# A scan whose steps share TensorE with the products around it: four layers on one core, and the end of the program rewritten

## The chip, the core and the metric

The kernel runs on one core of a Trainium2 chip. TensorE (PE, with its weight loads as PEld) multiplies and transposes, VectorE (DVE), ScalarE (ACT) and GpSimd (POOL) do the rest, and SyncE (SP) issues the DMAs. All data are fp32; a product shows in the records as two passes, each with its own weight load, a transpose as one. The metric is the device time of one execution in microseconds (us), median of the runs.

## What is computed

Sixteen sequences of 128 tokens with 256 features go through four layers, each with its own weights. The reference, cut to what matters here:

```python
x = L0(x, ctx, mask)      # self attention with a mask, gated memory, feed-forward (relu)
x = L1(ctx, x)            # two single-head attentions, a small feed-forward (gelu), norms
x = L2(x, ctx)            # causal cross attention, norm, feed-forward (gelu)
# L3:
x = x + mha(norm(x), norm(base_state))
U = (norm(x) @ W_in.T + b_in) @ Bmat                  # [16, 128, 64]
def step(s, u_t):
    s = silu(s @ A.T) + u_t                           # s: [16, 64]
    return s, s
_, states = scan(step, zeros, U)                      # 128 steps, one after another
x = x + states @ Cmat
mod = program_probs.mean(axis=1) @ W_prog.T + b_prog
return x + mod[:, None, :]
```

The scan is serial in the tokens: step t needs the state of token t-1, for all sixteen sequences together.

## The kernel before

The sixteen sequences are taken in pairs, so there are eight tiles (`NT = 8`) of 2 x 128 tokens. Each tile goes through streams of work named by a letter: H and A are layer 0, G the context, M layer 1, J and B layer 2, K and C layer 3. The order in which TensorE, VectorE, ScalarE and GpSimd take the steps of all streams is written out by hand in four long lists (`TENSOR_ORDER` and so on, in which `C7.mix` is the step "mix" of stream C for tile 7). The lists are the same in both kernels.

TensorE's results go round four PSUM banks (`work_bank_0` to `_3`). A step that fills a bank counts up the semaphore `filled`; the engine that empties it counts up that bank's `drained`. `open_bank` waits until the bank's last user has been emptied. Attention scores go to four more banks (`scores_bank`), which the waits on `maxed` and `exped` free.
The last steps of the main part are a chain for tile 7: `C7.turn` (transposes of attention weights), `C7.mix`, `C7.out` (L545), addition and norm on VectorE and GpSimd, `C7.flip.x7` (four transposes, L528), `C7.drive` (L723), which leaves the inputs of the scan in `u_all` [64, 128 tokens, 16 sequences].

Then comes the end of the program, which the change rewrites:

- TensorE first runs four products of the matrix A with all of `u_all` (L731), 32 tokens each, into the four scores banks: the silu of step t needs A times (silu state of t-1 plus u of t-1), and this is the second part of it.
- Sixteen products of one column (L739) give the means of the program probabilities, loaded into `prog` when `C7.drive` is done.
- For t = 2 to 127 a product of 64 rows, 64 columns of weights and 16 moving columns (L744) adds A times the state to the bank, and ScalarE writes the silu to `w_state` (L1126). They wait for each other in each step through `stepped` and `silued`.
- VectorE builds `stT`, whose upper half holds the means for all tokens (L1021) and whose lower half is silu plus u, 32 tokens at a time (L1029), the last quarter in four pieces.
- Sixteen products of 256 columns (L754) multiply `stT` with `w_last` (Cmat over W_prog), two to a bank; VectorE adds each bank to `x7` (L1038) and SyncE stores the pair (L495).

`stT`, `prog` and the hidden rows of the feed-forwards (`hT`) are one piece of memory, `hidden`; `w_state` lies in `probs`.

## Time and profile before

| | us |
| --- | --- |
| median of 3 runs | 937.99 (936.37 to 939.94) |
| profiled execution, its own time | 936.61 |
| its span | 934.5 |
| TensorE busy | 765.0 (82%) |
| VectorE, ScalarE, GpSimd busy | 550.1, 443.9, 336.5 |
| mean granted clock of TensorE | 0.907 of 2.4 GHz |
| start of the first wide product of the end (L731) | 827.81 |
| first and last product of the scan (L744) start | 838.27 and 920.77 |

A profile is one execution. Its span runs from the first to the last instruction, and its own time is 2.1 us longer. Lines of the page give an instruction group by source line, with busy time, mean length, and the idle time of its engine just before. The chain of waits goes back from the last instruction to what released each piece of work. Busy time of TensorE is no measure of its throughput, since its records overlap.

### The profile page before, as it was taken

The numbers are of one execution on the slowest core, as the hardware profiler recorded it, in microseconds if no ns is written. First come the engines' busy times: TensorE is split into PE (matmuls) and PEld (weight loads), VectorE is DVE, ScalarE is ACT, GpSimd is POOL, SyncE is SP. The second block draws the span as 40 slices with busy tenths as digits, with TensorE's granted clock in tenths as the row PEclk, the third lists the DMA queues.
The fourth block names the chain that finished last, engine by engine and source line by source line (L and its number), as shares of the span: only waits on it lengthen the run. The fifth ranks groups of instructions, "written<-read, shape, count | busy, mean of one in ns | idle before, by whom it ended". The sixth has DMA issues, their size and how long they took to land.

```text
span 934.5 us, 16718 instructions
## 1 busy us (share of the span) xinstructions
PE 765.0 (82%) x5520; PEld 617.2 (66%) x5520; DVE 550.1 (59%) x2244; ACT 443.9 (48%) x1776; POOL 336.5 (36%) x343
## 2 busy tenths in 40 slices
PE   0479798799899989998999999999889667575556
PEld 0368677688677868787787778877678546434445
DVE  0267767745977687678867885878763661320002
ACT  0184275536583667366536845683723631312221
POOL 3032444433644454354525551655343331200000
PEclk9999999899999999999999999999999888655556
DMA  8400100000000000000000000000000000010002
GB/s 321 156 7 2 29 1 18 13 1 1 13 7 12 2 12 7 13 13 2 7 13 12 1 1 13 2 1 1 2 1 1 1 1 1 1 22 1 1 0 90
DMA packets 14710, 18.75 MB, mean 20 GB/s; under 512 B 3485, under 2 KB 12194, under 8 KB 13986
## 3 DMA queue, kind: packets, MB, share of 16 engines
q1 hardware_dynamic: 14626, 17.69, 5.7%
q8 instruction: 45, 0.74, 0.3%
q14 instruction: 39, 0.32, 0.1%
HBM read 15.59 MB, written 2.10 MB: 19 GB/s over the span
## 4 chain that ended last, share of the span: by engine, by line
PE 60%; DVE 18%; ACT 10%; issue 6%; SPq 2%; POOL 2%; DMA 2%; DVEq 0%; POOLq 0%
PE work_bank L536 19%; PE work_bank L545 18%; ACT probs L1063 6%; PE scores_bank L744 5%; PE work_bank L674 4%; DVE probsT L985 3%; PE scores_bank L572 3%; DVE xn L902 3%; ACT probs L1126 3%; PE work_bank L594 2%; DVE stats L921 2%; PE work_bank L528 2%; DVE probs L884 2%; DMA bias<-in_mask 2%; PE work_bank L666 1%
## 5 line engine op out<-in xcount | busy, mean ns | idle before, releaser
L767 POOL TENSOR_TENSOR probs<-probs,rtotal 128x512 f32<-128x512 f32 x160 | 165.6, 1044 | 209.9 <-DVE rtotal L975 208.3
L1063 ACT ACTIVATE probs<-probs,nmx 128x128 f32<-128x128 f32 x512 | 197.9, 390 | 54.8 <-DVE nmx L884 54.5
L545 PE MATMUL work_bank<-L_w,hidden 128*128 128x256 f32 x512 | 114.8, 383 | 1.6 <-issue 1.0
L985 DVE COPY probsT<-work_bank 128x512 f32<-128x512 f32 x160 | 104.7, 681 | 11.5 <-PE work_bank L674 10.6
L767 POOL TENSOR_TENSOR rstd<-veps,half 128x2 f32<-128x2 f32 x64 | 44.8, 699 | 184.7 <-DVE veps L929 183.8
L545 PEld LDWEIGHTS work_bank<-L_w,hidden 128*128 128x128 f32 x512 | 97.2, 192 | 15.2 <-issue 1.6
L674 PE MATMUL work_bank<-ident,probs 128*128 128x128 f32 x640 | 94.1, 287 | 15.9 <-POOL probs L767 9.9
L674 PEld LDWEIGHTS work_bank<-ident,probs 128*128 128x128 f32 x640 | 73.8, 146 | 36.3 <-POOL probs L767 19.3
L1063 ACT ACTIVATION_READ_ACCUMULATOR probs<-probs,nmx 128x1 f32 x512 | 96.6, 189 | 0.0
L528 PE MATMUL work_bank<-ident,xn 128*128 128x128 f32 x256 | 42.6, 287 | 48.0 <-DVE xn L902 45.9
L744 PE MATMUL scores_bank<-probs,a_t 64*64 64x16 f32 x252 | 49.5, 275 | 33.4 <-ACT probs L1126 33.4
L884 DVE CUSTOM_DVE_ANT_0 probs<-scores_bank,causal 128x128 f32<-128x128 f32 x256 | 56.2, 285 | 20.6 <-PE scores_bank L572 20.0
L536 PE MATMUL work_bank<-B_actT,L_w 128*128 128x256 f32 x256 | 63.9, 403 | 5.3 <-DVE probsT L985 3.6
L528 PEld LDWEIGHTS work_bank<-ident,xn 128*128 128x128 f32 x256 | 30.0, 147 | 57.0 <-issue 49.1
L744 PEld LDWEIGHTS scores_bank<-probs,a_t 64*64 64x64 f32 x252 | 36.1, 202 | 46.7 <-ACT probs L1126 46.7
L884 DVE CUSTOM_DVE_ANT_0 probs<-scores_bank,bias 128x128 f32<-128x128 f32 x256 | 57.5, 283 | 7.8 <-PE scores_bank L572 7.5
L536 PE MATMUL work_bank<-A_actT,L_w 128*128 128x256 f32 x256 | 61.3, 390 | 0.0
L536 PEld LDWEIGHTS work_bank<-B_actT,L_w 128*128 128x128 f32 x256 | 50.2, 201 | 15.3 <-DVE B_actT L945 7.4
L536 PEld LDWEIGHTS work_bank<-A_actT,L_w 128*128 128x128 f32 x256 | 48.7, 195 | 8.6 <-issue 1.7
L1126 ACT ACTIVATE probs<-scores_bank 64x16 f32<-64x16 f32 x127 | 22.6, 178 | 62.4 <-PE scores_bank L744 62.4
L1029 DVE TENSOR_TENSOR hidden<-probs,u_all 64x128 f32<-64x128 f32 (+1 forms) x7 | 4.2, 641 | 78.6 <-ACT probs L1126 78.6
L1063 ACT ACTIVATE probs<-scores_bank,nmx 128x128 f32<-128x128 f32 x128 | 45.0, 390 | 6.8 <-DVE nmx L877 6.8
(162 smaller groups left out, 1424.9 us busy)
## 6 DMA issues: line engine op xcount, KB each, us to landing
L_w<-in_L_w SPq DMA_DIRECT2D x4, 1024.0 KB, 10.8
x_in<-in_x SPq DMA_DIRECT2D x8, 256.0 KB, 2.7
c_in<-in_ctx SPq DMA_DIRECT2D x8, 256.0 KB, 2.7
out<-x_all SPq DMA_DIRECT2D x8, 256.0 KB, 2.2
rows<-in_rows SPq DMA_DIRECT2D x1, 1280.0 KB, 8.0
bias<-in_mask SPq DMA_DIRECT2D x8, 128.0 KB, 2.2
L_wq<-in_L_wq SPq DMA_DIRECT2D x3, 256.0 KB, 9.7
L_wv<-in_L_wv SPq DMA_DIRECT2D x3, 256.0 KB, 10.2
```

Source lines behind the costliest of these rows:

```text
L528: mm = nc.tensor.transpose(d[:, c * PT + b * P:c * PT + b * P + P], src[:, b, c * P:c * P + P], ident[:])
L536: mm = nc.tensor.matmul(d[:, m * PT:m * PT + PT], w[:, k, (m0 + m) * P:(m0 + m) * P + P], xT[:, k, :], start=(k == 0), stop=(k == DC - 1))
L545: mm = nc.tensor.matmul(d[:, b * D:b * D + D], xT, w, start=(n == 0), stop=(n == len(todo) - 1))
L572: mm = nc.tensor.matmul(s_bank[g][:, c * 2 * P:(c + 1) * 2 * P], qT[s][of, c, b * P:b * P + P], kT[s][of, c, b].rearrange("p e t -> p (e t ...
L674: mm = nc.tensor.transpose(d[:, j * P:j * P + P], src[:, j, :], ident[:])
L744: mm = nc.tensor.matmul(s_bank[t // 32][0:SS, (t % 32) * B:(t % 32) * B + B], a_t[:], w_state[:, t - 1, :], start=False, stop=True, skip_g ...
L767: return nc.gpsimd.tensor_tensor(out, a0, a1, op)
L884: ins = nc.vector.tensor_tensor_reduce(out=e_at[slot][:, j, :], in0=d[:, j * P:j * P + P], in1=more, scale=-1.0, scalar=3.0e38, op0=ALU.ad ...
L902: nc.vector.tensor_scalar(norm_slot(s, i, key)[:, b, :], src[:, b, :], moments[:, n, b, 0:1], rstd[:, n, b:b + 1], ALU.subtract, ALU.mult) ...
L985: nc.vector.tensor_copy(turn_slot(s, i, key), d[:].rearrange("p (j k) -> p j k", j=4))\
L1063: ins = nc.scalar.activation(e_at[slot][:, j, :], src, ACT.Exp, bias=nmx[:, slot, j:j + 1], scale=1.0 if s == "C" else -1.0, accum_out=tot ...
L1126: nc.scalar.activation(w_state[:, t, :], s_bank[t // 32][0:SS, (t % 32) * B:(t % 32) * B + B], ACT.Silu)\
```

## The change

1. **Waits.** TensorE's waits go through a helper `ready`, which leaves out a wait that an earlier one of the same semaphore already covers. Where a step waited for several emptied banks, it waits only for the last one that each of VectorE and ScalarE empties (`emptied_last`).
2. **Means.** The sixteen mean products stand ahead of `C7.flip.x7` and go to a scores bank; their load is issued when the last feed-forwards have been read, and VectorE copies them after the last `flip`. The Silu table is loaded by a Silu of zeros after `C7.out`.
3. **Wide products.** Only the first stands ahead of the scan. The others stand behind steps 8, 40 and 72.
4. **The first 96 tokens** (`EARLY`) of each sequence are multiplied in halves of 128 columns (`early_part`), 32 products in all. From step 99 (`FROM`) on, one stands behind each step; three are left for after the scan. VectorE adds them two sequences at a time, and SyncE stores them so.
5. **The last 32 tokens** of four sequences are multiplied side by side in four 32-column tiles of the array. In steps 12 to 19 that is done with u and the means (`late_part`), and after the last step once more with the silu states read straight from `w_state`. Four DMAs move the residual of these tokens to `late`, where the four sequences of a group lie under each other; four DMAs store them, two from SyncE and two from ScalarE.

```diff
+EARLY, FROM = 96, 99
+        def emptied_last(fills):
+            out = []
+            for e in "da":
+                mine = [x for x in fills if x in EMPTIED[e]]
+                if mine:
+                    s, i, step = max(mine, key=EMPTIED[e].get)
+                    out.append(done(s, i, *step))
+            return out
...
-            sp.wait_ge(*done("C", NT - 1, "drive"))
+            sp.wait_ge(*filled_at("A", NT - 1, "ffn2"))
+            sp.wait_ge(*filled_at("B", NT - 1, "ffn2"))
             sp.dma_start(prog, a["prog"].rearrange("b s k -> s b k")).then_inc(prog_loaded, 16)
-            for j in range(NT):
-                sp.wait_ge(last_added, j + 1)
-                sp.dma_start(out[bass.ds(j * PAIR, PAIR)].rearrange("b s d -> s b d"), x7(j)).then_inc(out_stored, 16)
-            sp.wait_ge(out_stored, 16 * NT)
+            sp.wait_ge(*summed_at("C", NT - 1, "x7b"))
+            for j in range(4):
+                sp.dma_start(late[32 * j:32 * j + 32, :, :],
+                             x7_all[EARLY:P, :, :].rearrange("p (g j) d -> p g j d", j=4)[:, :, j, :])\
+                    .then_inc(late_moved, 16)
+            for n in range(NT):
+                sp.wait_ge(last_added, n + 1)
+                sp.dma_start(out[bass.ds(n * PAIR, PAIR), 0:EARLY].rearrange("b s d -> s b d"), x7(n)[0:EARLY])\
+                    .then_inc(out_stored, 16)
+            for j in (0, 1):
+                sp.wait_ge(late_added, 4)
+                sp.dma_start(out[:, EARLY:P].rearrange("(g j) s d -> j s g d", j=4)[j], late[32 * j:32 * j + 32])\
+                    .then_inc(out_stored, 16)
...
+            def ready(of, n):
+                if waited.get(of.name, 0) < n:
+                    waited[of.name] = n
+                    pe.wait_ge(of, n)
...
             def mix(s, i, step):
                 first = 4 * (step[1] if len(step) > 1 else 0)
-                for j in range(4):
-                    pe.wait_ge(*done(s, i, "turn", first + j))
-                pe.wait_ge(*done(KEYS[s], i, "v"))
+                for at in emptied_last([(s, i, ("turn", first + j)) for j in range(4)]):
+                    ready(*at)
+                ready(*done(KEYS[s], i, "v"))
...
+                if (s, i, step) == ("C", NT - 1, ("flip", "x7")):
+                    ready(exped, EXPED["C", NT - 1, ("exp", 3)])
+                    pe.wait_ge(prog_loaded, 16)
+                    for b in range(B):
+                        mm = nc.tensor.matmul(s_bank[3][SS:P, b:b + 1], prog[:, b, :], mean_w[:], start=True, stop=True)
+                    mm.then_inc(prog_meant, 1)
...
+            def late_part(k):
+                g, lo = k // 2, (k % 2) * P
+                for j in range(4):
+                    mm = nc.tensor.matmul(w_bank[g // 2][32 * j:32 * j + 32, (g % 2) * D + lo:(g % 2) * D + lo + P],
+                                          stT[:, 4 * g + j, EARLY:P], w_last[:, lo:lo + P], start=True, stop=True)
+                if k % 4 == 3:
+                    mm.then_inc(late_filled, 1)
+
+            def early_part(k):
+                b, lo = k // 2, (k % 2) * P
+                n = b // PAIR
+                if k % 4 == 0:
+                    if n < 2:
+                        pe.wait_ge(states_ready, 3)
+                    elif n < 4:
+                        pe.wait_ge(late_added, n - 1)
+                    else:
+                        pe.wait_ge(last_added, n - 3)
+                at = (b % PAIR) * D + lo
+                mm = nc.tensor.matmul(w_bank[(n + 2) % W_BANKS][0:EARLY, at:at + P], stT[:, b, 0:EARLY],
+                                      w_last[:, lo:lo + P], start=True, stop=True)
+                if k % 4 == 3:
+                    mm.then_inc(last_filled, 1)
...
-            for n in range(4):
+            mm = from_u(0)
             for t in range(1, P):
...
                 if t > 1:
                     pe.wait_ge(silued, t - 1)
                     mm = nc.tensor.matmul(s_bank[t // 32][0:SS, (t % 32) * B:(t % 32) * B + B], a_t[:],
                                           w_state[:, t - 1, :], start=False, stop=True, skip_group_check=True)
                 mm.then_inc(stepped, 1)
+                if t in (8, 40, 72):
...
+                    from_u(t // 32 + 1)
...
+                if 12 <= t < 20:
+                    late_part(t - 12)
+                if t >= FROM:
+                    early_part(t - FROM)
+
+            pe.wait_ge(silued, P - 1)
+            for g in range(4):
+                for j in range(4):
+                    mm = nc.tensor.matmul(s_bank[g // 2][32 * j:32 * j + 32, (g % 2) * D:(g % 2) * D + D],
+                                          w_state[:, EARLY:P, 4 * g + j], w_last[0:SS, :], start=True, stop=True)
+                if g % 2:
+                    mm.then_inc(late_filled, 1)
+            for k in range(P - FROM, 2 * B):
+                early_part(k)
```

How the instructions stand on the engines, first of the kernel before, then of the changed one. TensorE from `C7.mix` to the first scan steps, before; the names in brackets are the semaphores waited for:

```order
L594 MATMUL work_bank<-probsT,v 32x128 [waits drained_3,drained_2,drained_0,drained_1]
L594 MATMUL work_bank<-probsT,v 32x128 x15
L545 MATMUL work_bank<-L_wo,C_qT 128x256 [waits drained_1,drained_0]
L545 MATMUL work_bank<-L_wo,C_qT 128x256 x3
L528 MATMUL work_bank<-ident,xn 128x128 [waits normed,drained_2]
L528 MATMUL work_bank<-ident,xn 128x128
L528 MATMUL work_bank<-ident,xn 128x128 [waits normed]
L528 MATMUL work_bank<-ident,xn 128x128
L723 MATMUL work_bank<-C_actT,w_drive 64x256 [waits drained_3,drained_2]
```

```order
L731 MATMUL scores_bank<-u_all,a_t 64x496 [waits drained_3]
L731 MATMUL scores_bank<-u_all,a_t 64x512 x3
L739 MATMUL work_bank<-mean_w,hidden 64x1 [waits drained_3,drained_2,prog_loaded,drained_1,drained_0]
L739 MATMUL work_bank<-mean_w,hidden 64x1 x15
L744 MATMUL scores_bank<-probs,a_t 64x16 [waits silued] x126
```

The same stretch of TensorE in the changed kernel, up to the first late products:

```order
L629 MATMUL work_bank<-probsT,v 32x128 [waits drained_0,drained_3]
L629 MATMUL work_bank<-probsT,v 32x128 x15
L580 MATMUL work_bank<-L_wo,C_qT 128x256 [waits drained_1,drained_0]
L580 MATMUL work_bank<-L_wo,C_qT 128x256 x3
L664 MATMUL scores_bank<-mean_w,hidden 64x1 [waits prog_loaded,exped]
L664 MATMUL scores_bank<-mean_w,hidden 64x1 x15
L563 MATMUL work_bank<-ident,xn 128x128 [waits normed,drained_2]
```

```order
L772 MATMUL scores_bank<-u_all,a_t 64x496 [waits drained_3]
L806 MATMUL scores_bank<-probs,a_t 64x16 [waits silued] x7
L772 MATMUL scores_bank<-u_all,a_t 64x512
L806 MATMUL scores_bank<-probs,a_t 64x16 [waits silued] x4
L779 MATMUL work_bank<-w_last,hidden 32x128 [waits drained_3,drained_2,late_ready,drained_1,drained_0]
L779 MATMUL work_bank<-w_last,hidden 32x128 x3
L806 MATMUL scores_bank<-probs,a_t 64x16 [waits silued]
L779 MATMUL work_bank<-w_last,hidden 32x128 x4
```

The mean products have moved ahead of the transposes, three wide products into the scan, and `mix` waits for two semaphores instead of four.

TensorE from step 126 of the scan to the end of the program in the changed kernel:

```order
L806 MATMUL scores_bank<-probs,a_t 64x16 [waits silued]
L796 MATMUL work_bank<-w_last,hidden 96x128
L806 MATMUL scores_bank<-probs,a_t 64x16 [waits silued]
L796 MATMUL work_bank<-w_last,hidden 96x128 [waits last_added]
L825 MATMUL scores_bank<-w_last,probs 32x256 [waits silued]
L825 MATMUL scores_bank<-w_last,probs 32x256 x15
L796 MATMUL work_bank<-w_last,hidden 96x128 x3
```

Before, the scan's 126 products stood in a row and sixteen products of 256 columns behind them (L754, two for each wait); now one of 128 columns stands behind each of the last steps, and sixteen quarter-tile products and three of 128 columns behind the scan.

## Rows read from the trace of the kernel before

**Rows 1.** The page: granted clock in 40 slices, chain by engine, one costly group.

```profile
PEclk9999999899999999999999999999999888655556
...
PE 60%; DVE 18%; ACT 10%; issue 6%; SPq 2%; POOL 2%; DMA 2%; DVEq 0%; POOLq 0%
...
L744 PE MATMUL scores_bank<-probs,a_t 64*64 64x16 f32 x252 | 49.5, 275 | 33.4 <-ACT probs L1126 33.4
```

**Rows 2.** The chain that ended last, in order of time: start, length, what.

```profile
827.81 7.03 PE scores_bank L731 x8
834.84 3.50 PE work_bank L739 x32
838.35 0.33 PE scores_bank L744 x2
...
920.77 0.41 PE scores_bank L744 x2
...
921.92 9.27 PE work_bank L754 x32
931.21 0.69 DVE x_all L1038
```

**Rows 3.** Timeline of one scan step: start, length, engine, line, what, idle before.

```profile
871.93 0.28 PEld L744 LDWEIGHTS scores_bank<-probs,a_t 64*64 64x64 f32 x2 [0.38 <-ACT probs L1126]
871.93 0.39 PE L744 MATMUL scores_bank<-probs,a_t 64*64 64x16 f32 x2 [0.27 <-ACT probs L1126]
872.36 0.18 ACT L1126 ACTIVATE probs<-scores_bank 64x16 f32<-64x16 f32 x1 [0.48 <-PE scores_bank L744]
872.59 0.29 PEld L744 LDWEIGHTS scores_bank<-probs,a_t 64*64 64x64 f32 x2 [0.37 <-ACT probs L1126]
```

**Rows 4.** Stretches: length, busy PE, PEld, DVE, ACT, POOL, clock, DMA share, GB/s.

```profile
827.80:838.20 10.40, 10.39 (x40) 5.07 (x40) 0.00 (x0) 1.68 (x3) 0.00 (x0) 0.50 0.24 50
...
921.90:926.10 4.20, 4.17 (x10) 3.36 (x11) 1.81 (x5) 0.00 (x0) 0.00 (x0) 0.50 0.09 31
926.30:931.20 4.90, 4.88 (x23) 3.96 (x21) 3.56 (x6) 0.00 (x0) 0.00 (x0) 1.00 0.70 232
```

**Rows 5.** Timeline of TensorE's products, tile 7 of layer 3.

```profile
813.01 1.93 PE L594 MATMUL work_bank<-probsT,v 128*32 128x128 f32 x32 [1.09 <-DVE probsT L985]
815.75 3.78 PE L545 MATMUL work_bank<-L_wo,C_qT 128*128 128x256 f32 x8 [0.80 <-DVE C_qT L991]
823.09 1.09 PE L528 MATMUL work_bank<-ident,xn 128*128 128x128 f32 x4 [3.56 <-DVE xn L902]
```

**Rows 6.** DMA: two issues in a row on SyncE's queue, and one load.

```profile
3.15 0.43 SPq L467 DMA_DIRECT2D L_wv<-in_L_wv  x1
3.63 0.43 SPq L467 DMA_DIRECT2D L_wk<-in_L_wk  x1
...
hidden<-in_prog SPq DMA_DIRECT2D x1, 512.0 KB, 4.2
```

**Rows 7.** Timeline of VectorE in the scan.

```profile
838.59 1.22 DVE L1021 COPY hidden<-means 64x2048 f32<-64x2048 f32 x1
858.05 1.01 DVE L1029 TENSOR_TENSOR hidden<-probs,u_all 64x512 f32<-64x512 f32 x1 [18.23 <-ACT probs L1126]
```

**Rows 8.** Timeline of TensorE's weight loads where the tile shape changes.

```profile
832.93 0.23 PEld L731 LDWEIGHTS scores_bank<-u_all,a_t 64*64 64x64 f32 x1 [0.63 <-issue]
834.77 3.49 PEld L739 LDWEIGHTS work_bank<-mean_w,hidden 128*64 128x64 f32 x32 [1.61 <-issue]
```

**Rows 9.** Wait instructions of open_bank; stalls of mix; pieces of the chain at three stalls.

```profile
L503 PEldq EVENT_SEMAPHORE  x461: 51/51/3605, 38.3 to 823.3; - x154
...
  DVE probsT L985: 28.2, 12
...
423.08 0.14 issue
...
812.66 0.35 issue
...
815.71 0.04 issue
```

More of the change, by code:

```diff
@@ L253 @@
 FILL_AT = {x: n for n, x in enumerate(FILLS)}
+EMPTIED = {e: {x: n for n, x in enumerate(program(e)) if x in FILL_AT} for e in "da"}
 ROUND_AT = {x: n for n, x in enumerate(ROUNDS)}
@@ L511, in flip @@
                 elif key == "x4":
-                    pe.wait_ge(*done("M", i, "self"))
+                    ready(*done("M", i, "self"))
                     src = x4[:, i % 2]
                 elif key == "o":
-                    for b in range(PAIR):
-                        pe.wait_ge(*done("B", i, "mix", b))
+                    for at in emptied_last([("B", i, ("mix", b)) for b in range(PAIR)]):
+                        ready(*at)
                 else:
@@ L1024, in _ @@
[L1024 to L1033 removed]
+            nc.vector.tensor_copy(stT[SS:P, :, :], means[SS:P, :].unsqueeze(2).broadcast_to([SS, B, P]))
@@ new lines, in _ @@
+            dve.wait_ge(*done("C", NT - 1, "drive"))
+            nc.vector.tensor_copy(stT[0:SS, :, EARLY:P], u_all[:, EARLY:P, :].rearrange("p t b -> p b t"))\
+                .then_inc(late_ready, 1)
+            for k in range(2):
+                dve.wait_ge(late_filled, k + 1)
+                if k == 0:
+                    dve.wait_ge(late_moved, 16 * 4)
+                nc.vector.tensor_tensor(late[:, 2 * k:2 * k + 2, :], by_batch(w_bank[k]), late[:, 2 * k:2 * k + 2, :],
+                                        ALU.add).then_inc(late_added, 1)
@@ new lines, in add_late @@
+            def add_late(k):
+                dve.wait_ge(late_filled, k + 3)
+                if k == 0:
+                    dve.wait_ge(late_added, 2)
+                nc.vector.tensor_tensor(late[:, 2 * k:2 * k + 2, :], by_batch(s_bank[k]), late[:, 2 * k:2 * k + 2, :],
+                                        ALU.add).then_inc(late_added, 1)
+            whole = (P - FROM) // 4
+            for n in range(whole):
+                add_early(n)
+            for k in range(2):
+                add_late(k)
@@ L1040, in _ @@
+            for n in range(whole, NT):
+                add_early(n)
         @block.scalar
@@ L1120, in _ @@
                     ins.then_inc(free, 1)
[L1122 to L1123 removed]
+            act.wait_ge(*filled_at("C", NT - 1, "out"))
+            nc.scalar.activation(w_state[:, 0, :], zero[:], ACT.Silu)
             for t in range(1, P):
@@ L1127, in _ @@
                     .then_inc(silued, 1)
+            for j in (2, 3):
+                act.wait_ge(late_added, 4)
+                nc.scalar.dma_start(out[:, EARLY:P].rearrange("(g j) s d -> j s g d", j=4)[j],
+                                    late[32 * j:32 * j + 32]).then_inc(out_stored, 16)
 def _columns(inputs):
```

123 lines of the change are left out of this document (57 added, 66 removed).

## The prediction

> **What bounds the kernel now.** I read the page first: its chain of waits, its clock row, then the chain in order of time for the last 110 us. TensorE heads 60% of the chain, and its granted clock is 9 tenths or more until it falls to 5 for the last eighth of the program [rows 1]. That last part is the scan, and the chain in order of time shows what it is made of [rows 2]. After the last input of the scan is ready (827.8), TensorE runs four products of 496 or 512 columns (7.03 us) and sixteen products for the mean of the program probabilities (3.50 us), and only then the scan's second step begins, at 838.3. The last step begins at 920.77, 82.5 us later. Then come sixteen products of 256 columns (9.27 us), whose eight additions and stores run alongside, the last addition at 931.21, and the last store, with which the span ends at 934.5. One scan step takes 0.66 us [rows 3]: TensorE's loads start at 871.93, its product ends 0.39 later, ScalarE's Silu runs from 872.36 for 0.18, and the next load starts at 872.59. Nothing in a step is throughput. Its loads take 0.28 and its products are 16 columns wide, so the array itself is free some 0.15 to 0.2 us after the start and lies idle for half a microsecond. The change tries to fill that hole. All of it runs at 1.2 GHz, as the granted clock of 0.50 says [rows 4].
>
> **Terms of the sum, head.** The first step needs only the first of the four wide products, 7.03 / 4 = 1.76 us; with its latency and one Silu, the second step can start at about 827.81 + 1.9 + 0.25 = 829.98 instead of 838.35 - 0.08 = 838.27. That is -8.3 us. It needs the sixteen mean products out of the way. They now stand ahead of the last transposes of the main part, after the product that ends the attention. That product's eight records of 256 columns start at 815.75 and take 3.78, so the array is free at 819.2; the transposes start at 823.09 because VectorE and GpSimd normalise in between [rows 5]. The mean products need 3.50 in a hole of 3.9, less a change of shape of 0.14 (below): they fit by about 0.26 us. If they did not, the transposes and all behind them would move by the overshoot; I take 0, at most +0.3. Their input, a load of 4.2 us to landing [rows 6], is now issued right after the last feed-forward product instead of at the scan's start. VectorE's small copy of the means sits in its idle time before the last drive term. The copy of the means over all tokens (1.22 us) and the new copy of the inputs (like an addition of 64x512, 1.01 us) [rows 7] end at about 830.2, and the first late product waits for them only at step 12, about 837.
>
> **Wide products in the scan.** Three of 512 columns now stand behind steps 8, 40 and 72, same array shape as the step. Each streams 1.71 us (0.85 for a record, two records), from about 0.25 after the step's start, so the next step starts at about 1.97 instead of 0.66: 3 x 1.31 = +3.9 us. So of the 5.3 us removed ahead of the scan, 3.9 come back.
>
> **Products of another shape in the scan.** Here the price is in what TensorE does when the tile shape changes. In the wide products the loads run one ahead of the products, one each 0.85 us. The load at 832.93 is the last of them; its product starts one record later, at 833.79, and streams until 834.64. The next load, for a 128x64 tile after 64x64 ones, is not taken ahead and comes only at 834.77 [rows 8]: a change of shape costs 0.13 after the end of the stream, and the load ahead is lost. Each inserted product changes shape twice, since the step is 64x64, the late products 128x32 and the early ones 128x128 tiles. The Trainium skill says the same in "TensorEngine Tiling (Array Packing)", Key Properties: changing the tiling mode, not just the tile, drains the engine. It speaks against this change, and the price here is taken from the rows alone.
>
> An **early step** (steps 99 to 127, 29 products of 128 columns with 96 rows of output): the step's second record starts at 0.13 (0.39 [rows 3] less a record's 0.26 to 0.28 [rows 1]), the shape has changed at 0.30, the load and the first start-up take 0.06 to 0.13, two records stream 0.213 each (half of the 0.43 for 256 columns, from 3.78 for eight [rows 5]), and the change back takes 0.14. The next step starts at 0.93 to 1.03. I take 1.00, nearer the upper end because the group of eight records [rows 5] shows 0.16 of start-up beyond its eight streams and the latency. That is +0.34 on each of 28 intervals: +9.5 us (7.6 to 10.4). The bound below is 0, if the product fitted the hole; it is a real bound, as the hole is 0.5 wide and the product's stream 0.43.
>
> A **late step** (12 to 19, eight groups of four 32-column tiles): the mix product shows four such tiles at work together, 32 records of 128 columns in 1.93 [rows 5], so a group of eight records streams 0.43, with 0.05 of stagger. The next step starts at about 0.92: 8 x 0.26 = +2.1 us. VectorE's early additions, 0.69 each [rows 2], come once in four steps and wait for nobody on the path.
>
> **Tail.** Now from the start T of the last step. Before, the last addition starts at T + 10.44 and the span ends at T + 13.7. After: the early product of that step and the change of shape until T + 1.02; sixteen products of 64x32 tiles, four at a time, 256 columns, 4 x 0.85 = 3.41 and another change of shape until T + 4.6; the three early products that are left over, 6 x 0.213 with start-up and latency until T + 6.3; one addition of 0.69: T + 7.0. Then SyncE issues three stores, where before it issued one; back to back they start 0.47 apart with cold queues [rows 6], about 0.42 at the 0.37 that stores take, so the end comes 2.6 + 0.8 = 3.4 after the addition: T + 10.4. That is -3.3 us.
>
> **Waits.** The helper `ready` drops waits that an earlier one covers; the built program has 262 wait instructions on TensorE instead of 680 (461 of the old ones are those of one line, `open_bank`) [rows 9]. A wait instruction costs 0.05 and stands 0.1 before the next. While the array is busy the sequencer runs ahead and it costs nothing. Where TensorE stands still for the result, it costs: with three of them the mix starts 0.35 after the copy it waited for, with one 0.14, with none 0.04 [rows 9]. The mix's loads stood still for that copy 12 times: 12 x 0.3 = 3.6. Some 25 other stalls lose one wait each: 25 x 0.08 = 2.0. Ceiling 5.6; floor 0, since no wait is added there (VectorE, ScalarE or GpSimd may be what is late next). TensorE heads 60% of the chain, so I take 0.6 x 5.6 = -3.5.
>
> **Sum:** -8.3 + 3.9 + 9.5 + 2.1 - 3.3 - 3.5 = +0.4 us on a span of 934.5 in a run of 936.6. The three timed runs have a median of 938.0, 1.4 above it; I add the sum to the median: **938.4 us**. What the head and the tail give, the steps in the scan take back.
>
> **Rivals.** (1) *The clock rises in the early steps.* TensorE will have no idle gap for 29 us. For it: in the tail of before it was busy without a gap at 0.50 from 921.9, and the clock was 1.00 from 926.3 on [rows 4]. Against it: from 827.8 to 838.2 it was busy all the time too, and stayed at 0.50 [rows 4]; those were 64x64 and 128x64 tiles, the tail's were 128x128. In an early step the 128x128 tiles stream for 0.43 of 1.0. At 2.4 GHz the inserted product fits the hole: -9.5, and the end's streams halve, -2.5: 926.4. The Trainium skill's "TensorE: Matmul & The Clock Gate", Why this matters for your kernels, advises to leave no idle gaps to stay at full clock; the row from 827.8 shows that this is not enough here. (2) *The early product mostly hides* in the Silu's time, because its load is taken ahead after all, or the waits give their whole ceiling: -5 to -9: 931. (3) *Slower: a full drain on each change of shape.* The step's product has a latency of 0.39, of which I let only 0.30 pass before the next shape's load, and after the early product 0.14 instead of the 0.2 or more of a record's latency. With 0.11 more on each of two changes in 36 steps: 72 x 0.11 = +8: 946. It decides from an early step of about 1.15 us upwards. (4) *The waits bring nothing*, because another engine is late next: +3.5: 941.9, still no difference. (5) *The quarter tiles do not run side by side* with these operands: +1.3 in each of 8 late steps and +10 in the tail: 959.
>
> **How the numbers follow.** A measurement of this kernel can tell about 0.5%, 4.7 us, from no change. Forecast 0.47 (a small part of it below 933.3), rival 1 0.10, rival 2 0.10, rival 3 0.15, rival 4 0.15, rival 5 0.03. Faster by over 0.5%: 0.10 + 0.10 + 0.02 = 0.22. Within: 0.45 + 0.15 = 0.60. Slower: 0.15 + 0.03 = 0.18. The range leaves out rivals 1 and 5 and the far part of 3: 928.0 to 946.5.
>
> **What would show it.** The second step starts 2.2 us after the first wide product does; the transposes before the last drive term start within 0.3 us of when the normalised rows are ready; steps 20 to 98 stay at 0.66; steps with a wide product take 1.97, late steps 0.92, early steps 1.00 at a granted clock of 0.50; from the last step's start to the end 10.4 us; up to the last drive term the program is 3.5 us shorter. Early steps at 0.66 or 1.2 us, or a clock of 1.00 in them, would make the prediction wrong, and so would a main part that did not move or that moved by 6 us and more.

## The result, and the profile after

| | before | after |
| --- | --- | --- |
| median, us | 938.01 (8 runs, 935.03 to 939.94) | 942.91 (8 runs, 941.16 to 944.66) |
| ratio, 95% interval | | 1.0049 (1.0032 to 1.0065) |
| span of the profiled execution | 934.5 | 939.7 |
| start of the last drive term (`u_all`) | 827.28 | 828.80 |
| from there to the end | 107.2 | 110.9 |
| last scan step starts | 920.77 | 929.09 |

The forecast was 938.4 us, in a range of 928.0 to 946.5. The kernel is slower by 0.32 to 0.65%, so it lies on the edge of what the text called no change. In the profiled executions the sum of the end of the program came out (+3.7 us measured, +3.9 forecast). The main part did not get 3.5 us shorter, it got 1.5 us longer.

The page of the kernel after: the clock row, and the chain by engine. Against [rows 1] the clock no longer comes back to 6 in the last slice, and TensorE heads 62% of the chain instead of 60%.

```profile
PEclk9999999999999999999999999999999888555555
...
PE 62%; DVE 18%; ACT 9%; issue 5%; SPq 2%; DMA 2%; POOL 1%; DVEq 0%; POOLq 0%
```

The chain of the kernel after in order of time (start, length, what), which answers to [rows 2]:

```profile
817.29 3.78 PE work_bank L580 x8
821.07 3.50 PE scores_bank L664 x32
...
824.63 1.10 PE work_bank L563 x4
...
828.80 0.48 DVE u_all L1089
...
829.33 1.92 PE scores_bank L772 x2
...
831.51 0.41 PE scores_bank L806 x2
...
859.82 0.39 PE scores_bank L806 x2
860.21 1.79 PE scores_bank L772 x2
862.40 0.41 PE scores_bank L806 x2
...
901.67 0.67 PE work_bank L796 x2
902.34 0.32 PE scores_bank L806 x2
902.67 0.67 PE work_bank L796 x2
...
929.49 0.67 PE work_bank L796 x2
930.16 3.58 PE scores_bank L825 x32
933.73 1.54 PE work_bank L796 x6
935.29 0.69 DVE x_all L1116
```

The means (L664) now lie in the hole ahead of the transposes (L563): these start 7.34 us after the product of `out` does, 824.63 - 817.29, just as before (823.09 - 815.75, [rows 5]). The hole is filled to the brim, though: the last mean product ends at 824.57, 0.06 before the transposes start, and the chain runs through it. The scan starts 8.3 us sooner after its inputs. In the early steps the ScalarE rows are gone from the chain: TensorE alone sets their pace, 902.67 - 901.67 = 1.00 less rounding (0.993 over 28 intervals). The timeline of one such step of the kernel after (start, length, engine, line, what, idle before) shows where it goes:

```profile
901.60 0.39 PEld L796 LDWEIGHTS work_bank<-w_last,hidden 128*96 128x96 f32 x2
901.60 0.74 PE L796 MATMUL work_bank<-w_last,hidden 128*96 128x128 f32 x2
901.71 0.18 ACT L1220 ACTIVATE probs<-scores_bank 64x16 f32<-64x16 f32 x1 [0.48 <-PE scores_bank L806]
902.27 0.29 PEld L806 LDWEIGHTS scores_bank<-probs,a_t 64*64 64x64 f32 x2 [0.28 <-issue]
```

The silu is finished at 901.89, 0.38 before the next step's load, and that load stands behind the foreign product. The granted clock, in the stretches of the early steps and of the tail of the kernel after (length, busy time of each engine, clock, DMA share, GB/s), to be read against [rows 4]:

```profile
901.70:929.10 27.40, 27.40 (x111) 18.63 (x111) 4.12 (x6) 4.98 (x28) 0.00 (x0) 0.50 0.16 44
929.10:935.30 6.20, 6.16 (x43) 3.27 (x42) 2.08 (x4) 0.18 (x1) 0.00 (x0) 0.50 0.12 32
```

TensorE is busy for 27.40 of 27.40 us and stays at 1.2 GHz.

### The profile page after: what moved, and what is told of

Same layout as the page of the kernel before. It is cut to its first block, busy times and chain, and to the rows that moved or that the text cites. A ratio compares the mean times of both kernels' runs of the same rounds, so it can differ in the third digit from the quotient of the medians.

```text
span 939.7 us, 16569 instructions
## 1 busy us (share of the span) xinstructions
PE 783.9 (83%) x5648; PEld 624.8 (66%) x5648; DVE 553.0 (59%) x2245; ACT 444.0 (47%) x1776; POOL 336.4 (36%) x344
## 4 chain that ended last, share of the span: by engine, by line
PE 62%; DVE 18%; ACT 9%; issue 5%; SPq 2%; DMA 2%; POOL 1%; DVEq 0%; POOLq 0%
PE work_bank L571 20%; PE work_bank L580 18%; PE scores_bank L806 5%; ACT probs L1157 5%; PE work_bank L715 4%; DVE probsT L1060 3%; PE scores_bank L607 3%; DVE xn L977 3%; PE work_bank L563 2%; PE work_bank L796 2%; PE work_bank L629 2%; DVE stats L996 2%; DVE probs L959 2%; DMA bias<-in_mask 2%; ACT probs L1220 2%
## 5 line engine op out<-in xcount | busy, mean ns | idle before, releaser
L1060 DVE COPY probsT<-work_bank 128x512 f32<-128x512 f32 x160 | 104.5, 680 | 11.6 <-PE work_bank L715 10.9
L563 PE MATMUL work_bank<-ident,xn 128*128 128x128 f32 x256 | 42.7, 287 | 46.5 <-DVE xn L977 44.0
L563 PEld LDWEIGHTS work_bank<-ident,xn 128*128 128x128 f32 x256 | 30.0, 147 | 54.7 <-issue 42.2
L1082 DVE TENSOR_SCALAR hidden<-work_bank,cols 128x256 f32<-128x256 f32 x64 | 27.3, 474 | 28.4 <-PE work_bank L571 28.3
```

The lines of the kernel that those rows point to most:

```text
L563: mm = nc.tensor.transpose(d[:, c * PT + b * P:c * PT + b * P + P], src[:, b, c * P:c * P + P], ident[:])
L1060: nc.vector.tensor_copy(turn_slot(s, i, key), d[:].rearrange("p (j k) -> p j k", j=4))\
```

## Experiments

### The two halves of the change apart

`e1_waits` is the kernel before with nothing but the dropped waits (267 wait instructions on TensorE instead of 680):

```diff
+                if waited.get(of.name, 0) < n:
+                    waited[of.name] = n
+                    pe.wait_ge(of, n)
-                    pe.wait_ge(drained[n % W_BANKS], n // W_BANKS)
+                    ready(drained[n % W_BANKS], n // W_BANKS)
...
-                    for b in range(PAIR):
-                        pe.wait_ge(*done("B", i, "mix", b))
+                    for at in emptied_last([("B", i, ("mix", b)) for b in range(PAIR)]):
+                        ready(*at)
```

> The kernel before with the dropped TensorE waits alone (267 wait instructions instead of 680), the end of the program as before. Theory A (the waits gave nothing, because each stall shortened at TensorE is given back at the next wait for another engine): 938.0, between 936.5 and 939, ratio 1.000; in the trace the mix after its copy starts 0.2 to 0.3 us earlier and the next stall takes it back. Rival (my forecast of the waits): 934.5, ratio 0.996. Rival (the missing waits cost something, through another order of events): 939.5 or more.

`e2_end` is the kernel after with all the waits put back:

```diff
-            out = []
-            for e in "da":
-                mine = [x for x in fills if x in EMPTIED[e]]
-                if mine:
-                    s, i, step = max(mine, key=EMPTIED[e].get)
-                    out.append(done(s, i, *step))
-            return out
+            return [done(s, i, *step) for s, i, step in fills]
...
-                if waited.get(of.name, 0) < n:
-                    waited[of.name] = n
-                    pe.wait_ge(of, n)
+                pe.wait_ge(of, n)
```

> The changed kernel with all of TensorE's waits put back (675 wait instructions), so the new end of the program alone. Theory A: the end costs +3.8 by my sum, +3.7 by the profile after, from the last drive term on: 941.8, ratio 1.004. If the waits had helped by 3.5 and something else had lost 4.7, this would be 946.

Measured, both against the kernel before on the same chip (940.14): e1_waits 939.26, ratio 0.9998 (0.998 to 1.0016); e2_end 941.11, ratio 1.002 (0.9998 to 1.0041). In the trace of e2_end the stretch from the last drive term to the end is 3.6 us longer than before (110.8 against 107.2). So the new end costs what its sum said, by the trace; the medians allow -0.2 to +3.9 us. The dropped waits bring nothing that can be measured: the interval of e1_waits runs from -1.9 to +1.5 us and leaves out the forecast's -3.5.

### Why an early step takes 0.99 us

`e4_same_shape` gives the early products the tile of the step itself:

```diff
-                mm = nc.tensor.matmul(w_bank[(n + 2) % W_BANKS][0:EARLY, at:at + P], stT[:, b, 0:EARLY],
-                                      w_last[:, lo:lo + P], start=True, stop=True)
+                mm = nc.tensor.matmul(w_bank[(n + 2) % W_BANKS][0:SS, at:at + P], stT[0:SS, b, 0:SS],
+                                      w_last[0:SS, lo:lo + P], start=True, stop=True)
```

> The changed kernel, but each early product uses 64 rows and 64 tokens only, so it has the tile shape of the scan step (64x64) and the same 128 moving columns and stream of 0.427 us. It leaves out the means and tokens 64 to 95 of the first part. Theory (the two changes of shape are what makes an early step 0.993): the early steps fall to 0.66 to 0.72 us. Rival (the stream of 0.43 itself does not fit between product and Silu): they stay above 0.85.

`s1_rows64` changes only the rows of that tile to 64 (96 columns stay), `s2_tokens64` only its columns (128 rows stay):

```diff
 s1_rows64:
-                mm = nc.tensor.matmul(w_bank[(n + 2) % W_BANKS][0:EARLY, at:at + P], stT[:, b, 0:EARLY],
-                                      w_last[:, lo:lo + P], start=True, stop=True)
+                mm = nc.tensor.matmul(w_bank[(n + 2) % W_BANKS][0:EARLY, at:at + P], stT[0:SS, b, 0:EARLY],
+                                      w_last[0:SS, lo:lo + P], start=True, stop=True)
 s2_tokens64:
-                mm = nc.tensor.matmul(w_bank[(n + 2) % W_BANKS][0:EARLY, at:at + P], stT[:, b, 0:EARLY],
+                mm = nc.tensor.matmul(w_bank[(n + 2) % W_BANKS][0:SS, at:at + P], stT[:, b, 0:SS],
```

> The kernel after with the early products on 64 rows of weights instead of 128; the columns stay at 96, so the tile is 64x128 and the step's 64x64. The means' part of these tokens is left out. If any change of tile shape costs the step its 0.33 us, the early steps stay at 0.99. If only a change in the number of rows does, they go to 0.66 to 0.75.

> The kernel after with the early products on 64 columns of weights (64 tokens) instead of 96; the rows stay at 128, so the tile is 128x64 and the step's 64x64. The tokens 64 to 95 are left out. If any change of tile shape costs the step its 0.33 us, the early steps stay at 0.99. If only a change in the number of columns does, they go to 0.66 to 0.75.

One early step of each in the chain in order of time, first e4_same_shape, then s1_rows64, then s2_tokens64:

```profile
914.81 0.51 PE work_bank L796 x2
915.32 0.15 PE scores_bank L806 x2
```

```profile
915.06 0.67 PE work_bank L796 x2
915.73 0.32 PE scores_bank L806 x2
```

```profile
914.96 0.62 PE work_bank L796 x2
915.58 0.32 PE scores_bank L806 x2
```

The step takes 0.66 us in e4_same_shape, 0.99 in s1_rows64 and 0.94 in s2_tokens64. The product streams the same 128 columns twice in all three. So the third of a microsecond is no streaming time: with the step's own tile the product is free. Nor is it the length of the weight load, since s2_tokens64 loads 64 columns as e4_same_shape does. Changing the rows alone or the columns alone brings back nearly all of it. All three leave out a part of the sum, so only their times are read. (One execution each; the step is read from 28 intervals, all alike but for the first one of e4_same_shape, 0.70.)

`e3_from128` leaves the wide and the late products in the scan and puts all 32 early ones behind it:

```diff
-EARLY, FROM = 96, 99
+EARLY, FROM = 96, 128
```

> The changed kernel with no early product between the steps: all 32 stand behind the scan. The steps 99 to 126 go back from 0.993 to 0.660: -9.3 us. The 29 products move to the end: at 1.2 GHz 29 x 0.427 = +12.4, so 945.9 in sum; if the clock rises to 2.4 GHz after some 4 us of them, as it did in the end of the kernel before, about +8.5 and 942. Theory: inserting the early products is close to neutral against running them behind the scan, because each costs 0.333 us in the scan and 0.21 to 0.43 behind it.

Measured: 940.23 us, ratio 1.0005 (0.9988 to 1.0022) where the kernel after had 1.0049; the expectation, 942 to 946, was too high. From the last step to the end it takes 18.4 us instead of 10.6 (+7.9), and 28 steps are 0.33 us shorter (-9.3). So putting the early products between the steps loses 1.4 us against running them behind the scan. The two ratios are 4 us apart; where the rest of that lies was not found. Its tail, in stretches (columns as in [rows 4]), is busy almost in full at 1.2 GHz for 9 us and then gets 2.4 GHz, as in the kernel before:

```profile
922.30:931.70 9.40, 9.13 (x58) 6.79 (x59) 2.76 (x4) 0.18 (x1) 0.00 (x0) 0.50 0.21 51
932.00:938.50 6.50, 4.29 (x40) 4.08 (x38) 4.08 (x6) 0.00 (x0) 0.00 (x0) 1.00 0.71 199
```

### Where the dropped waits' gain went

Set beside each other product by product, the main parts of before and of e1_waits drift apart at each `mix` for which TensorE stood still: the product starts 0.3 to 0.5 us earlier. At the next transposes, which wait for VectorE's norm, 0.3 of it is given back. By 436 us the lead was 0.8 us in e1_waits and 0.55 in the kernel after. Of that, 0.5 and 0.1 had stood there since the first products at 36 us, so 0.3 to 0.5 us had been gained. Then both e1_waits and the kernel after lose it at once. The chain in order of time there, for before:

```profile
453.49 2.18 DMA bias<-in_mask
...
455.69 0.04 DVE bias L934
```

and for the kernel after:

```profile
452.94 3.90 DMA bias<-in_mask
...
456.87 0.04 DVE bias L1009
```

The mask load of the last tile starts 0.55 us earlier and lands 1.2 us later (456.84 against 455.67). VectorE stands idle in front of it, and from there on the kernel after is 1.1 us behind before, and e1_waits 1.0. The DMA queues between issue and landing, for before (453.4 to 455.7) and then for the kernel after (452.9 to 456.9):

```profile
q1 hardware_dynamic: 272, 0.13, 20.5%
q14 instruction: 1, 0.01, 1.3%
```

```profile
q1 hardware_dynamic: 272, 0.13, 11.9%
q8 instruction: 1, 0.02, 1.5%
q14 instruction: 1, 0.01, 0.8%
```

The load carries the same 272 packets; in the kernel after one more instruction fetch falls into its time. This load took 3.5 to 4.1 us in all eight traces with dropped waits, the six with the mask operation in its old place (after, e1, e3, e4, s1, s2) and the two with it moved (w1, b3), and 2.1 to 2.2 in all six with the waits kept. Each of the fourteen traces has six such loads from 62 us on, 84 in all. In ten of them a fetch of queue q8 starts within the first 1.8 us, and these took 3.0 to 4.1 us; the other 74 took 2.0 to 2.3, two of them with a fetch that starts 2.0 us after the issue. Two of the ten stand in kernels that keep their waits: b1_one_shape at 149.78 us (3.5) and x1_waits_thrice at 372.85 (3.0). So it goes with the fetch and not with the dropped waits as such. Near the last load such a fetch starts at 459.9 us in before, behind the landing, and at 454.6 in the kernel after, inside it. The fetch itself was not moved by an experiment; the waiting for the load was.

In `m1_mask_later` VectorE's mask operation of tiles 2 to 7 stands 4 to 15 operations later (13 to 15 in all but the first), so that no load of it is waited for; `w1_waits_mask` is the same with the waits dropped:

```diff
-A4.turn.2 A4.turn.1 C1.norm.x7 A4.max.5 A4.rec.4 A4.max.6 A4.max.7 A4.rec.5 G6.bias A4.rec.6 B2.ffn2 C1.flip.x7
+A4.turn.2 A4.turn.1 C1.norm.x7 A4.max.5 A4.rec.4 A4.max.6 A4.max.7 A4.rec.5  A4.rec.6 B2.ffn2 C1.flip.x7
...
-A4.turn.7 M3.flip.cr C2.norm.x6 A4.mix.1 H5.flip.x M3.max.s C2.flip.x6 G4.norm.c M3.rec.s A4.out M3.turn.s A4.stat.x2
+A4.turn.7 G6.bias M3.flip.cr C2.norm.x6 A4.mix.1 H5.flip.x M3.max.s C2.flip.x6 G4.norm.c M3.rec.s A4.out M3.turn.s A4.stat.x2
```

> The kernel before with one thing moved: VectorE's mask operation of the pairs 2 to 7 (bias<-bias, L934 in the kernel before) stands some 8 operations later in its order, behind the last transposed weights of the pair two earlier, so that it no longer stands and waits for its 128 KB mask load. In the trace of before VectorE stood idle ahead of 7 of these 8 operations for 33.1 us, always until the load bias<-in_mask. If these waits are on the path that sets the end, the main part gets shorter by up to 6 x 2.2 us (the load's time from issue to landing where nothing disturbs it), 937.99 - 13 = 925; a part of it comes back at the next stall, so 2 to 8 us of gain, 930 to 936. If what VectorE loses there is made good at the next wait for another engine, as the dropped waits were, the time is unmoved: 938 +-1.5, ratio 0.998 to 1.002.

> The kernel before with the dropped TensorE waits (as in e1_waits) and VectorE's mask operation moved as in m1_mask_later. It is to be set against m1_mask_later. Theory A, the gain of the dropped waits (0.6 to 0.9 us by 434 us) was eaten by the mask load that came down late at 453 us (3.9 us from issue to landing instead of 2.2): then with no engine waiting for that load the dropped waits are worth 0.5 to 2 us here, ratio to m1_mask_later 0.998 to 0.9995. Theory B, what the dropped waits save is given back at the next stall whatever the load does: no difference to m1_mask_later, within 0.1%. Theory C, the extra stretch at granted clock 0.50 near 526 us belongs to the dropped waits: then it is here again and this kernel is slower than m1_mask_later by about 1.7 us.

Measured: m1_mask_later 936.28, ratio 0.9975 (0.9955 to 0.9995); w1_waits_mask 935.94, ratio 0.9986 (0.9966 to 1.0006). VectorE's idle time ahead of the mask operation, in before and then in m1_mask_later:

```profile
  DMA bias<-in_mask: 33.1, 7
```

```profile
  DMA bias<-in_mask: 23.8, 2
```

Five waits of some 2 us are gone, but the gain is 0.5 to 4 us by the interval, and 0.4 by the two spans. Of the five loads only two, at 62.55 and 453.49, had stood in the chain of before at all. At the second of them the chain of m1_mask_later shows what was almost as late as the load, TensorE's products:

```profile
451.94 3.47 PE work_bank L545 x16
...
455.44 0.47 DVE B_cur L1003
```

And with the collision out of the way the dropped waits still bring nothing that shows (0.9986 against 0.9975, 1.0011 of m1_mask_later). Theory A of the expectation, 0.998 to 0.9995, is not borne out; with intervals of 0.002 to either side it is not excluded either. The stretch that theory C expected is missing: at 526 us w1_waits_mask has the granted clock 1.00.

What remains is seen product by product. From 380 to 647 us, with both kernels at the same granted clock, w1_waits_mask gains 0.2 us on m1_mask_later in each 89 us, the turn of one tile, and b3_all (below) the same on b2_one_shape_mask. Over the nine turns of the main part that makes an estimate of 0.2 x 9 = 1.8 us. But w1_waits_mask comes to 104.5 us with another pattern of stalls, and there it has only half the clock. First m1_mask_later, then w1_waits_mask:

```profile
104.50:111.00 6.50, 4.68 (x56) 4.03 (x57) 5.70 (x19) 1.39 (x5) 1.70 (x3) 1.00 0.01 3
```

```profile
104.50:111.10 6.60, 5.97 (x50) 5.17 (x50) 4.95 (x17) 0.90 (x5) 1.72 (x3) 0.50 0.00 0
```

This costs it about 2 us. The profiled execution took 940.04 us; nine of the twelve took 934.4 to 938.3, at a mean clock of 0.903 to 0.908 where the profiled one has 0.900. So the stretch may belong to the execution and not to the kernel. In e1_waits such a stretch stands at another place, where before has 1.00 (first e1_waits, then before):

```profile
526.30:529.50 3.20, 3.20 (x15) 2.08 (x17) 1.68 (x17) 1.02 (x3) 1.04 (x1) 0.50 0.00 0
```

```profile
526.30:529.50 3.20, 3.20 (x43) 2.49 (x42) 2.35 (x18) 2.61 (x6) 0.21 (x1) 1.00 0.01 3
```

In the kernel after, this stretch costs 1.7 us too: its lag behind before goes from 1.0 to 2.7 us. But before loses the same elsewhere. From 769.2 to 779.4 us it has 1.2 GHz throughout and the kernel after for a third of that, and the lag falls by 1.5 us (first before, then the kernel after):

```profile
769.20:779.40 10.20, 7.96 (x21) 5.59 (x20) 2.72 (x9) 0.84 (x2) 3.23 (x3) 0.50 0.01 2
```

```profile
769.20:779.40 10.20, 6.17 (x22) 4.09 (x22) 5.43 (x15) 0.00 (x0) 4.50 (x4) 0.83 0.00 0
```

The table adds up the time at 1.2 GHz before the last drive term starts, from each trace's record of the granted clock (us):

| kernel | TensorE waits | last drive term starts | of it at 1.2 GHz | mask load of tile 7 |
| --- | --- | --- | --- | --- |
| before | all | 827.3 | 75 | 2.2, waited for |
| e2_end | all | 827.4 | 75 | 2.1, waited for |
| b1_one_shape | all | 825.4 | 67 | 2.1, waited for |
| m1_mask_later | all | 826.8 | 75 | not waited for |
| b2_one_shape_mask | all | 827.4 | 75 | not waited for |
| x1_waits_thrice (below) | tripled | 851.8 | 82 | 2.2, waited for |
| after | dropped | 828.8 | 74 | 3.9, waited for |
| e1_waits | dropped | 828.5 | 74 | 4.1, waited for |
| e4_same_shape | dropped | 829.4 | 77 | 3.7, waited for |
| e3_from128 | dropped | 831.3 | 80 | 3.7, waited for |
| s2_tokens64 | dropped | 830.8 | 80 | 3.5, waited for |
| s1_rows64 | dropped | 830.3 | 84 | 3.7, waited for |
| w1_waits_mask | dropped | 829.9 | 87 | not waited for |
| b3_all | dropped | 827.3 | 80 | not waited for |

e3, e4, s1 and s2 have the main part of the kernel after, instruction for instruction. Their last drive terms start 0.6 to 2.5 us later, with 3 to 10 us more at the lower clock. So the clock moves from one execution to the next too, by about as much as the waits could bring. Every timed execution has its mean granted clock on record. The 29 of before that were run beside e1_waits have 0.898 to 0.911 and times of 942.7 to 935.5 us; their average is 0.904, that of the 12 of e1_waits 0.905. On average, then, the dropped waits have not lowered the clock.

### What a wait instruction costs when there are more

`x1_waits_thrice` issues each wait of TensorE's main part three times:

```diff
+            def thrice(*at):
+                for _ in range(3):
+                    pe.wait_ge(*at)
...
-                    pe.wait_ge(drained[n % W_BANKS], n // W_BANKS)
+                    thrice(drained[n % W_BANKS], n // W_BANKS)
```

> The kernel before with each TensorE wait of the main part issued three times, the second and third on a value that is already there: some 1300 wait instructions more, where the change dropped 418. Theory A, a wait instruction costs 0.1 us where TensorE stands still for the result, and some of that reaches the end: with the same price as in the forecast, 0.6 x 5.6 for 418 waits, 1300 more cost 0.6 x 5.6 x 1300 / 418 = 10 us, 948, ratio 1.011; at the ceiling 17 us, 955. Theory B, what a wait costs at one stall is given back at the next, which waits for another engine: less than 3 us, ratio under 1.003. Each mix stall itself starts its product some 0.6 us later in either theory; the two differ in what the distance from the start to the last drive term shows.

Measured: 961.04 us, ratio 1.0251 (1.0222 to 1.028). The built program has 2176 wait instructions on TensorE, 1496 more. The last drive term starts 24.6 us later, at 851.8: 0.016 us for each, more than the forecast's ceiling gave (5.6 us for 418 waits, 0.013 each); 7 us more at 1.2 GHz are in it. Nearly half of it stands in one row of TensorE's waits, the mix products held back by the sequencer alone (us in total, times, longest); in before the like row of L594 has 1.0 us in 4 times.

```profile
PE work_bank L600 <- issue: 12.5, 15, 2.5
```

So a wait instruction has its price on the path, theory A, and the price of the forecast was no fiction. Yet from 680 downwards there was little left to save: 0.2 us in 89, and not the 0.4 that the forecast's 3.5 over nine turns would be. So the price of a wait is not one number: adding waits cost more for each than dropping them gave back.

### An end in which every product has the step's shape

`b1_one_shape` keeps the waits and the moved means, and cuts every product in the scan to 64 rows and 64 columns of weights: the wide ones in 24 pieces behind steps 2 to 25, the means' part of the last projection behind steps 33 to 64 (on rows 64 to 127), the states' part of the first 96 tokens behind steps 98 to 127; the last 32 tokens four side by side as in the kernel after, on states to which VectorE has added u first.

```diff
+            def halves(k, rows, count):
+                b, lo = k // 2, (k % 2) * P
+                at = (b % PAIR) * D + lo
+                for h in (0, SS):
+                    mm = nc.tensor.matmul(w_bank[(b // PAIR) % W_BANKS][h:h + SS, at:at + P], stT[rows, b, h:h + SS],
+                                          w_last[rows, lo:lo + P], start=True, stop=True)
...
+                if 2 <= t < 26:
+                    from_u((t - 2) // 8 + 1, (t - 2) % 8)
...
+                if MODS <= t < MODS + 32:
+                    mod_part(t - MODS)
+                if t >= FROM:
+                    early_part(t - FROM)
```

> All waits as before, and an end of the program that puts every product between the scan's steps in the step's own shape, 64 rows by 64 columns of weights: the three wide products in 24 pieces of 64 columns, one behind each of the steps 2 to 25; the means' part of the last projection in 64 products of 64 rows and 64 tokens, two behind each of the steps 33 to 64; the states' part of the first 96 tokens in 60 such products behind the steps 98 to 127 and 4 behind them; the last 32 tokens as in the kernel after, 16 products of 64 rows and 32 tokens, four side by side. If the shape change is what cost the steps 0.33 us each in the kernel after, all 127 steps stand 0.66 apart: the scan takes 83.9 us, first step 0.9 us after the last drive term, last step to the end about 8.5 to 10.5 us; against the kernel before (106.7 us from the last drive term to the end) 93.5 to 95.5 us, that is 11 to 13 us less, 925 to 927. If it is the foreign product by itself that costs (any pair of products behind a step), the steps with two products stay at 0.8 to 1.0 and 62 of them cost 9 to 20 us more: 934 to 946.

Measured: 925.68 us, ratio 0.9861 (0.9822 to 0.99). The steps stand 0.66 apart (124 of 125 intervals are within 0.04 of it, one is 0.75), and 86 of them carry foreign products, 62 of these two; from the last step to the end 9.7 us. From the last drive term to the end it takes 95.0 us, 12.2 less than before. One figure of the expectation was wrong: the second step begins 2.7 us after the drive term starts and not 0.9 after its end, since the first wide product (1.92) still stands ahead of it. The clock does not rise here either, in a stretch of early steps (columns as in [rows 4]):

```profile
893.00:912.00 19.00, 19.00 (x176) 14.65 (x176) 5.47 (x10) 4.96 (x28) 0.00 (x0) 0.50 0.24 65
```

`b2_one_shape_mask` adds the moved mask operation, `b3_all` the dropped waits as well.

> b1_one_shape with VectorE's mask operation moved as in m1_mask_later. The two edits lie in different parts of the program, so their gains should add: the ratio of b1_one_shape times that of m1_mask_later, 919 to 927 if both hold, and the ratio of b1_one_shape alone if the mask's wait is made good elsewhere.

> b2_one_shape_mask with TensorE's waits dropped as in the kernel after (about 418 fewer). If the dropped waits bring nothing also here, as w1_waits_mask against m1_mask_later, the ratio is that of b2_one_shape_mask, 0.981 to 0.985 of the kernel before (920 to 924). If they bring their forecast 3.5 us once nothing else is in the way, 0.979 or less.

Measured: 923.2 us, ratio 0.9827 (0.9799 to 0.9856), and 923.06 us, ratio 0.9847 (0.982 to 0.9873). The intervals of the three overlap. By their ratios each beats both kernels, the one before by 13 to 16 us and the one after by 17 to 21; the dropped waits add nothing here either.

## Why the prediction was right in all but one step

- **Head, -8.3.** Right. 2.2 us from the first wide product's start to the second step: 831.51 - 829.33 = 2.18. The means in the hole ahead of the transposes: no cost, 7.34 us in both, but without the 0.26 us to spare that the sum had.
- **Wide products, +3.9.** Right: the interval behind one is 1.98 us, three times. The next interval is 0.61, 0.05 shorter than a normal one, so +3.8.
- **Late steps, +2.1.** Right: 0.91 in eight intervals, +2.0.
- **Early steps, +9.5.** Right in size, 28 x 0.33 = +9.3, and in cause, as e4_same_shape and b1_one_shape showed: the price is the change of shape. Rival 3 (a full drain, over 1.15 us) and the part of rival 2 in which the product hides are out.
- **Tail, -3.3.** T + 10.6 measured against T + 10.4, and 13.7 before: -3.1.
- **Clock.** Rival 1 is out: 27.4 us without a gap at 0.50.
- **Waits, -3.5.** This is the step that failed. The change as a whole shows +1.5 in the main part, e1_waits by itself no difference (0.9998). The stalls shrank as said, 0.3 to 0.5 us at a mix. The ceiling counted each stall by itself, and 0.6 of it was taken because TensorE heads 60% of the chain (0.6 x 5.6 is 3.4, not 3.5). That share says nothing of what the next stall waits for. In the trace the next stall behind most of them is one for VectorE's norm, and it gives 0.3 back. At equal clock an estimated 1.8 us are left over the main part, half of the term. The lag of the kernel after behind before shows where even these went: -0.1 us at the first products, -0.55 at 436 us, +1.1 behind the last tile's mask load, +1.5 at the last drive term. The load alone makes +1.6. What comes behind it adds 0.4 in all, the stretches at half the clock (75 us in sum in before, 74 in the kernel after) and what the waits still give taken together. Rival 4 (the waits bring nothing, 941.9) is what happened, nearly: 942.91.
- **By its own signs** the prediction failed here: it named a main part that did not move as a sign of being wrong. The total lies 4.5 us above the forecast and inside the range because the range is 18.5 us wide; the parts of the end, each within 0.2 us, are no luck.

What stays open: how a fetch delays a load, and whether moving the fetch alone would give the 1.6 us back; and whether the dropped waits change the clock at all. In the table five of the eight kernels with dropped waits have 80 us and more at 1.2 GHz and none of those with the waits as before has over 75. But s1_rows64 and the kernel after differ by 10 us with one and the same main part, and over all executions e1_waits has the mean clock of before. These are single executions against averages; no run decides it.

## What to carry to other kernels

Before a product is put into the hole of a latency-bound loop on TensorE, cut it to the tile shape of the loop: with the same rows and columns of weights even two products of 128 columns were free, with each of the four other shapes tried (128x96, 64x96, 128x64 and four of 128x32 side by side) it cost 0.25 to 0.33 us a turn. Do not multiply a stall's saving by its engine's share of the chain; look for what the next stall waits for, and take the saving only if that is not another engine, and if it is small beside the scatter of single executions (here some 7 us, mostly with the granted clock) don't expect to see it in one trace. Likewise, five waits of VectorE, 2 us each, were worth 0.5 to 4 us once taken away: three were in no chain, and behind the last another engine was nearly as late.

## What the runs showed of the hardware

The step's product and a foreign one on the other half of the rows were taken together. In b1_one_shape the step uses rows 0 to 63 and the means' part rows 64 to 127 (timeline, steps at 851.95 and 852.61):

```profile
851.95 0.29 PE L804 MATMUL scores_bank<-probs,a_t 64*64 64x16 f32 x1
851.96 0.18 PEld L773 LDWEIGHTS work_bank<-w_last,hidden 64*64 64x64 f32 x2
851.96 0.48 PE L773 MATMUL work_bank<-w_last,hidden 64*64 64x128 f32 x2
```

The foreign product starts 0.01 us after the step's. The Trainium skill's "TensorEngine Tiling (Array Packing)", Key Properties, says that changing the tiling mode drains the engine; s1_rows64 and s2_tokens64 agree, with 0.33 and 0.28 us a step for two changes.

A 128 KB mask load took 3.0 to 4.1 us where a 16 KB instruction fetch of queue q8 started within its first 1.8 us (ten loads), and 2.0 to 2.3 elsewhere (74 loads).

The chip granted 1.2 GHz for the whole of 27.4 us in which TensorE was busy without a gap (kernel after) and for 19.0 us of b1_one_shape. In the tails of before and e3_from128, whose large products follow each other directly, it granted 2.4 GHz from 926.3 and about 932 on ([rows 4], and the rows of e3_from128). TensorE without a gap was not enough.
